# Second expert stage: finished rows scattered by POOL into a table in token order, read back by plain DMAs

## Chip, cores and metric

One core of a Trainium2 chip runs the whole program in one launch. The metric is the device time of an execution in microseconds (us), the median of three runs. Everything is fp32 (matmul operands are split into a high and a low part).

## The reference, cut to what matters

x is 8 x 1024 tokens of 128 values. A mixture-of-experts layer, a state-space mixer and a second mixture-of-experts layer follow one another, each with a residual:

```python
x = x + 0.5 * ffn(layernorm(x), router_w, w_gate, w_up, w_down)
x = x + attn(layernorm(x), ...)          # the mixer: conv, scan over time, gate, projection
x = x + 0.5 * ffn(layernorm(x), router_w, w_gate, w_up, w_down)

def ffn(x, ...):                         # 8 experts, each token goes to 2 of them
    logits = xt @ router_w.T
    topk_vals, topk_idx = jax.lax.top_k(logits, 2)
    g = sigmoid(topk_vals); g = g / (g.sum(-1) + 1e-10)
    for e in range(8):
        ge = sum(where(topk_idx == e, g, 0), -1)
        out += ge[:, None] * ((silu(xt @ w_gate[e]) * (xt @ w_up[e])) @ w_down[e])
```

The change concerns the last line of the program, the second ffn.

## The kernel before

A tile is 128 tokens, one on each partition; there are 64 of them, and x lives in SBUF (`x_sb`, its normed form in `xn_sb`). Three blocks follow each other: `first_stage` (first expert layer), `mixer`, `last_stage` (second expert layer, from 983 us on).

An expert layer works on groups of tiles. `LAYER2` has four groups of 24, 16, 16 and 8 tiles. For each group the router finds each token's two experts and gives both copies of the token a row in a buffer in DRAM where the rows of an expert lie together, in slots of 128 rows (`x_dispatched`). POOL writes the rows there by indirect DMAs (`Router.scatter`, L605: two a tile, each 128 rows of 512 B). The experts then work on pairs of slots (`Experts`), 28, 20, 20 and 12 pairs a group, 80 in all; the last pair of a group has one slot, so there are 156 slots. Slots are padded: 156 x 128 rows hold 16384 tokens' copies.

A step i of `pe_step`, `act_step` and `dve_step` is a software pipeline: gate and up matmuls of pair i (L714 to L716), silu (ACT L744), the product (DVE L770), turning the hidden rows of pair i - 1 (PE L724, ACT L751, DVE L778), turning the input rows of pair i + 2 (PE L703, ACT L758, DVE L785), the down matmuls of pair i - 2 (L736, L737) and its output rows (ACT L764, DVE L793 in `out_rows`). SP loads the input rows of a pair into one of four buffers (L664, it runs some five steps ahead of PE) and stores the finished rows to `y_dispatched`, still in expert order (L669, two buffers `yr`). Each engine runs its own queue strictly in order.

When all pairs of a group are stored, `Combine` brings the rows back: for each tile POOL issues two gathers (L380), one for each expert of its tokens, each 128 rows of 512 B by the row numbers in `row`; DVE adds each times its gate to x (L388, L391). Tile t may be gathered when tile t - 2 has landed and tile t - 4 has been added, and no sooner than `FETCH[t]`: pair 34 for tile 0, one tile a pair after that, so 46 tiles fall due before pair 80 and the rest after it. SP stores x to `out` in eight pieces of eight tiles, all of them queued behind its last store of output rows (L1752).

In `last_stage` POOL's queue is: the x scatters of groups 2 and 3 (24 tiles, 48 DMAs, one tile a pair from pair 10), then the 128 gathers. The same scatters of groups 0 and 1 are done in `mixer`.

## Time and profile before

| | us |
|---|---|
| median of 3 runs (lowest, highest) | 1322.62 (1321.95, 1323.84) |
| the profiled execution | 1321.73 |
| its span in the trace | 1320.0 |

| busy in the span | PE | DVE | ACT | POOL |
|---|---|---|---|---|
| us | 1078.9 | 901.4 | 768.8 | 540.9 |
| share | 82% | 68% | 58% | 41% |

The profile lists the busy time of each engine, the span cut into slices, the chain of work that ended last, and groups of instructions. A line number such as L605 is that of the kernel before. The whole-span shares say little here, since the three blocks have different limits; the trace is read by stretches. The silu of a pair (L744) marks its step: one silu a pair, so its start times are the pace of the expert loop. Pair 10's starts at 1028.01, pair 41's at 1131.01, pair 61's at 1198.68 and the last one, pair 79's, at 1258.61.

### The profile page before, as it was taken

Reading aid. Unit: us, or ns where it says so; the run is one execution under the profiler, and the core shown is the slowest. Engines: PE = TensorE matmul, PEld = TensorE weight load, DVE = VectorE, ACT = ScalarE, POOL = GpSimd, SP = SyncE. Lnnn points to the kernel's source line nnn. Section 1 sums busy time; section 2 is a strip of 40 time slices with the busy share of each in tenths; the row PEclk is TensorE's granted clock in tenths of the full one; section 3 lists DMA queues with packets and bytes.
Section 4 is the critical chain, followed back from the end, with each engine's and each line's share of the span. In section 5 each row is a group of like instructions: output and inputs, shape, how many; then the busy total and the mean of one; then the engine's idle time right before and its main releaser. Section 6 shows DMA issues by size and latency. Waiting matters only on the chain. (4 is left out here: it accounts for less than half of the span.)

```text
span 1320.0 us, 23316 instructions
## 1 busy us (share of the span) xinstructions
PE 1078.9 (82%) x6351; PEld 898.4 (68%) x6351; DVE 901.4 (68%) x2699; ACT 768.8 (58%) x1987; POOL 540.9 (41%) x595
## 2 busy tenths in 40 slices
PE   3578989998988999989989878986858999898820
PEld 3467877877866777767767666764637878777720
DVE  7667677768634778786868677567856775777742
ACT  5345655545548786877777747765625665454510
POOL 3615445654023333332223235530630465555565
PEclk9979999999989999999989889997879999999965
DMA  8535354444240000000000000001232344444352
GB/s 263 168 118 196 118 167 141 146 139 133 67 159 21 17 19 18 19 15 15 17 13 17 13 21 33 28 21 41 96 144 61 98 120 124 115 116 114 105 159 74
DMA packets 134330, 114.41 MB, mean 87 GB/s; under 512 B 15424, under 2 KB 118336, under 8 KB 134080
## 3 DMA queue, kind: packets, MB, share of 16 engines
q1 hardware_dynamic: 108864, 64.71, 16.4%
q0 software_dynamic: 16384, 33.59, 8.6%
q10 hardware_dynamic: 8960, 14.63, 3.2%
q8 instruction: 59, 0.97, 0.3%
q14 instruction: 63, 0.52, 0.1%
HBM read 52.90 MB, written 59.97 MB: 86 GB/s over the span
## 5 line engine op out<-in xcount | busy, mean ns | idle before, releaser
L605 POOL DMA_INDIRECT x_dispatched<-xn_sb,row x256 | 250.5, 979 | 259.5 <-DVE row L569 110.4
L380 POOL DMA_INDIRECT f_y_in<-y_dispatched,row x160 | 151.3, 946 | 115.1 <-issue 56.0
L953 POOL TENSOR_TENSOR x_skip<-tok,d_skip 128x256 f32<-128x256 f32 x64 | 40.9, 640 | 318.3 <-DVE y L1385 174.0
L1002 PE MATMUL bank<-xT_high,wc_high 128*128 128x512 f32 x256 | 129.3, 505 | 3.8 <-DVE xT_low L1311 3.1
L380 POOL DMA_INDIRECT y_in<-y_dispatched,row x96 | 95.1, 991 | 37.3 <-issue 19.8
L1002 PE MATMUL bank<-xT_high,wc_low 128*128 128x512 f32 x256 | 104.1, 407 | 0.0
L1002 PE MATMUL bank<-xT_low,wc_high 128*128 128x512 f32 x256 | 104.1, 407 | 0.0
L770 DVE TENSOR_TENSOR f_hf<-f_sg,banks 128x512 f32<-128x512 f32 x84 | 56.3, 670 | 61.5 <-issue 30.5
L736 PE MATMUL bank<-shared,f_hh 128*128 x326 | 92.5, 359 | 0.1
L744 ACT ACTIVATE f_sg<-banks 128x512 f32<-128x512 f32 x84 | 49.1, 585 | 70.8 <-PE banks L716 56.9
L1370 DVE TENSOR_TENSOR state<-state_decayed,bank 128x256 f32<-128x256 f32 x56 | 23.6, 421 | 91.4 <-PE bank L1071 88.1
L736 PE MATMUL bank<-shared,e_hh 128*128 x312 | 84.7, 348 | 0.0
L1193 ACT ACTIVATE da_masked<-upto,da 128x128 f32<-128x128 f32 x256 | 81.2, 392 | 0.7 <-DVE da L1337 0.7
L770 DVE TENSOR_TENSOR e_hf<-e_sg,banks 128x512 f32<-128x512 f32 x80 | 53.7, 671 | 40.8 <-ACT e_sg L744 21.7
L744 ACT ACTIVATE e_sg<-banks 128x512 f32<-128x512 f32 x80 | 47.2, 590 | 57.0 <-PE banks L716 37.3
L1069 PEld LDWEIGHTS bank<-x_dt,mix 128*128 128x128 f32 x512 | 74.3, 210 | 5.0 <-issue 1.0
L714 PE MATMUL banks<-shared,f_xh 128*128 x163 | 74.0, 454 | 2.9 <-DVE f_xl L785 1.3
L724 PE MATMUL bank<-ident,f_hf 128*128 128x128 f32 x326 | 52.9, 286 | 27.6 <-DVE f_hl L778 21.5
L737 PE MATMUL bank<-shared,f_hl 128*128 x326 | 75.2, 231 | 0.0
L1053 PE MATMUL banks<-da_masked,after 128*128 128x512 f32 x128 | 72.3, 649 | 1.7 <-ACT da_masked L1193 1.7
L724 PEld LDWEIGHTS bank<-ident,f_hf 128*128 128x128 f32 x326 | 41.0, 147 | 46.1 <-issue 23.1
L1069 PE MATMUL bank<-x_dt,mix 128*128 128x64 f32 x512 | 70.9, 286 | 0.0
(281 smaller groups left out, 3370.6 us busy)
## 6 DMA issues: line engine op xcount, KB each, us to landing
f_xr<-x_dispatched SPq DMA_DIRECT2D x79, 128.0 KB
y_dispatched<-f_yr SPq DMA_DIRECT2D x79, 128.0 KB
e_xr<-x_dispatched SPq DMA_DIRECT2D x76, 128.0 KB
y_dispatched<-e_yr SPq DMA_DIRECT2D x76, 128.0 KB
w_split<-shared ACTq DMA_DIRECT2D x8, 768.0 KB
shared<-w_split SPq DMA_DIRECT2D x8, 768.0 KB
x_dispatched<-xn_sb,row POOLq DMA_INDIRECT x256
out_dram<-x_sb SPq DMA_DIRECT2D x8, 512.0 KB
```

What stands on the lines that cost most here:

```text
L380: nc.gpsimd.indirect_dma_start(out=self.y_in[n % 4][k][:], out_offset=None, in_=self.rows[t], in_offset=bass.IndirectOffsetOnAxis(ap=row[k ...
L605: nc.gpsimd.indirect_dma_start(out=xd_dram[g.x_home], in_=xn_sb[:, t, :], in_offset=None, out_offset=bass.IndirectOffsetOnAxis(ap=row[k][: ...
L714: pe.matmul(to, high, w[:, 0:2 * H], start=True, stop=False)
L724: last = pe.transpose(b_h[:, (2 * u + c) * P:(2 * u + c + 1) * P], self.hf[i % 2][:, u, c * P:(c + 1) * P], ident[:])
L736: pe.matmul(to, self.hh[i % 2][:, 2 * u + c, :], w[:, at:at + 2 * D], start=(c == 0), stop=False)
L737: last = pe.matmul(to[:, 0:D], self.hl[i % 2][:, 2 * u + c, :], w[:, at:at + D], start=False, stop=(c == 1))
L744: nc.scalar.activation(self.sg[i % 2][:, 0:n, :], b_gu[i % 2][:].rearrange("p (u f) -> p u f", u=2)[:, 0:n, 0:H], ACT.Silu).then_inc(self. ...
L770: nc.vector.tensor_tensor(self.hf[i % 2][:, 0:n, :], self.sg[i % 2][:, 0:n, :], b_gu[i % 2][:].rearrange("p (u f) -> p u f", u=2)[:, 0:n, ...
L1002: last = pe.matmul(acc[:], wc[w][:, tap, k * P:(k + 1) * P], xTb[x][:, at:at + 512], start=(tap == 0 and i == 0), stop=(tap == CONV_K - 1 ...
L1053: pe.matmul(b_seg[:], after[:], dam[t % 2][:].rearrange("p h i -> p (h i)"), start=True, stop=True).then_inc(s_sg, 1)
L1069: pe.matmul(b_y[:, h * HD:(h + 1) * HD], mm[i][:, h, :], xdt[i][:, h, :], start=True, stop=True)
L1193: last = nc.scalar.activation(dam[t % 2][:, h, :], upto[:], ACT.Copy, scale=da[b % 2][:, c, h:h + 1])
```

## The change

Nothing changes in what is computed. In the second expert stage:

- Each row of `xn_sb` and of `x_dispatched` is 130 values wide instead of 128 (`XW`), in the first stage too. Column 128 holds 2 x token - 4N and column 129 the number of the expert that is the token's first choice, both written by two more DVE instructions a group in `choose`; they are zero in the first stage and in padding rows.
- When a pair's input rows are in SBUF, `targets` (two DVE instructions on 128 x 2 values, the second waits for the first) computes for each row its place in a table `y_by_token` of 2N rows: 2 x token + (1 if this expert is the token's first choice). Padding rows get a place beyond the table.
- `send` replaces the store by SP: POOL scatters the finished rows of each slot into the table, one indirect DMA a slot with a bounds check that drops rows beyond the table: 156 DMAs. Pair i's wait for its targets, its finished rows and the landing of pair i - 2's. There are four `yr` buffers instead of two; `out_rows` of pair i waits for the landing of pair i - 4's.
- The x scatters of groups 2 and 3 stand in POOL's queue between the sends: 16 tiles over steps 10 to 41, 8 tiles over steps 41 to 61.
- `Gathered` replaces `Combine`: SP reads the table in token order by 32 plain DMAs of 256 KB (two tiles each, four buffers), no gathers; DVE does the same two additions a tile. Before pair 80 come 55 tiles, one a step from step 34 on and two a step in steps 75 to 80; the 8 tiles of the last group and tile 55 come after the loop.
- `out` is stored piece by piece within SP's queue, not all at the end.

```diff
-                    last = nc.scalar.activation(xn_sb[:, t, :], x_sb[:, t, :], ACT.Identity,
+                    last = nc.scalar.activation(xn_sb[:, t, 0:D], x_sb[:, t, :], ACT.Identity,
...
                 if k == 0:
+                    if self.by_token:
+                        c(nc.vector.tensor_copy(xn_sb[:, tiles, D], token2[:, tiles]))
+                        c(nc.vector.tensor_scalar(xn_sb[:, tiles, D + 1], work2, -1.0, E + 1.0, ALU.mult, ALU.add))
...
             def load(self, sp, i):
                 need(sp, self.s_tr, i - XB + 1)
+                if self.router.by_token:
+                    need(sp, self.s_to, 2 * (i - XB + 1))
...
+            def targets(self, dve, i):
+                dve.wait_ge(self.s_xr[i % XB], 16 * (i // XB + 1))
+                if i >= 2 * YB:
+                    dve.wait_ge(self.s_yo[i % YB], self.sent(i - 2 * YB))
+                n = self.live(i)
+                rows = self.xr[i % XB]
+                if i:
+                    dve.wait_ge(self.s_to, 2 * i)
+                nc.vector.tensor_tensor(self.first[:, 0:n], rows[:, 0:n, D + 1], self.router.slotf[:, 2 * i:2 * i + n], ALU.is_equal
+                                        ).then_inc(self.s_to, 1)
+                dve.wait_ge(self.s_to, 2 * i + 1)
+                nc.vector.scalar_tensor_tensor(out=self.to[i % (2 * YB)][:, 0:n], in0=rows[:, 0:n, D], scalar=float(NOWHERE),
+                                               in1=self.first[:, 0:n], op0=ALU.add, op1=ALU.add).then_inc(self.s_to, 1)
+
+            def send(self, pool, i):
+                pool.wait_ge(self.s_to, 2 * i + 2)
+                pool.wait_ge(self.s_y, i + 1)
+                if i >= 2:
+                    pool.wait_ge(self.s_yo[(i - 2) % YB], self.sent(i - 2))
+                for u in range(self.live(i)):
+                    nc.gpsimd.indirect_dma_start(out=y_token, in_=self.yr[i % YB][:, u, :], in_offset=None,
+                                                 out_offset=bass.IndirectOffsetOnAxis(ap=self.to[i % (2 * YB)][:, u:u + 1], axis=0),
+                                                 bounds_check=2 * N - 1, oob_is_err=False
+                                                 ).then_inc(self.s_yo[i % YB], 16)
...
             def out_rows(self, dve, i):
                 dve.wait_ge(self.s_ylow, i + 1)
-                need(dve, self.s_yo[i % 2], 16 * (i // 2))
+                if not self.router.by_token:
+                    need(dve, self.s_yo[i % 2], 16 * (i // 2))
+                elif i >= YB:
+                    dve.wait_ge(self.s_yo[i % YB], self.sent(i - YB))
...
                 if i + 2 < self.pairs:
                     self.x_low(dve, i + 2)
+                    if self.router.by_token:
+                        self.targets(dve, i + 2)
...
+        class Gathered:
+            def load(self, sp, n):
+                sp.wait_ge(self.s_both, self.ADDED + max(0, 2 * (n - self.BUFS + 1)))
+                at = 4 * P * n
+                sp.dma_start(self.y_in[n % self.BUFS][:], y_token[at:at + 4 * P, :].rearrange("(t p k) d -> p t (k d)", p=P, k=2)
+                             ).then_inc(self.s_back[n % self.BUFS], 16)
...
+            SETTLED = 4
+            AHEAD = 6
+            LANDING = 2
             FETCH = []
             for g in LAYER2:
+                for n in range(g.first // 2, g.end // 2):
+                    FETCH.append(max(g.pair_end + SETTLED, FETCH[-1] + (1 if g.index > 1 else 2) if FETCH else 0))
+            SENT = {}
+            for g, first, end in ((LAYER2[2], beside[0].known, LAYER2[2].pair - 7), (last, LAYER2[2].pair - 7, last.pair - 7)):
                 for t in range(g.first, g.end):
+                    SENT.setdefault(first + (t - g.first) * (end - first) // g.tiles, []).append((g, t))
...
                 @block.gpsimd
                 def _(pool):
                     setup.wait_filled(pool, 6)
-                    for g in LAYER2[2:]:
-                        for t in range(g.first, g.end):
-                            r.scatter_paced(pool, ex, g, t, FIRST_SENT + t - LAYER2[2].first)
-                    for g in LAYER2:
-                        ex.wait_stored(pool, g.pair_end)
-                        for t in range(g.first, g.end):
-                            if FETCH[t] < PAIRS2:
-                                pool.wait_ge(ex.s_gu, FETCH[t] + 1)
-                            combine.pool(pool, t)
+                    for i in range(PAIRS2 + 2):
+                        for g, t in SENT.get(i, ()):
+                            r.scatter(pool, g, t)
+                        if i >= 2:
+                            ex.send(pool, i - 2)
```

## Rows read from the trace of the kernel before

**Rows 1.** Busy time by stretch, the last block: engine busy (instructions), clock, DMA share, GB/s.
```profile
core 0: us, PE busy (x) PEld busy (x) DVE busy (x) ACT busy (x) POOL busy (x), PEclk, DMA share, GB/s
985.00:1028.00 43.00, 37.20 (x231) 31.58 (x231) 28.66 (x96) 23.72 (x54) 0.00 (x0) 0.89 0.23 66
1028.00:1129.00 101.00, 96.38 (x635) 82.46 (x636) 71.35 (x174) 57.98 (x133) 57.35 (x60) 1.00 0.40 116
1129.00:1195.00 66.00, 58.80 (x380) 49.93 (x379) 48.43 (x116) 33.40 (x81) 36.96 (x40) 1.00 0.44 118
1195.00:1257.00 62.00, 55.91 (x362) 47.52 (x363) 46.39 (x112) 30.52 (x73) 34.98 (x37) 1.00 0.39 105
1265.56:1320.00 54.44, 0.00 (x0) 0.00 (x0) 13.88 (x40) 0.00 (x0) 32.30 (x35) 0.50 0.44 123
```

**Rows 2.** The chain that ended last, from 1250 us: its shares, and late pieces (start, us, what).
```profile
by line: issue 28.6%; DMA f_y_in<-y_dispatched,row 26.3%; POOL f_y_in L380 24.0%; another core or an unknown queue 4.4%; POOLq L1742 1.7%; DVE x_sb L391 1.0%; DVE e_hl L778 1.0%; PE bank L736 0.9%; ACT e_sg L744 0.9%; PE bank L724 0.9%; DVE
...
1267.35 5.04 DMA f_y_in<-y_dispatched,row
1274.37 4.98 DMA f_y_in<-y_dispatched,row
...
1313.19 2.43 DMA f_y_in<-y_dispatched,row
```

**Rows 3.** DVE in order of time: last output rows, last gathered tile.
```profile
1265.28 0.28 DVE L793 TENSOR_TENSOR e_yr<-bank,e_yl 128x128 f32<-128x128 f32 x1
...
1315.65 0.35 DVE L388 SCALAR_TENSOR_TENSOR x_sb<-f_y_in,gate,x_sb 128x128 f32<-128x128 f32 x1 [1.62 <-DMA f_y_in<-y_dispatched,row]
1316.04 0.35 DVE L391 SCALAR_TENSOR_TENSOR x_sb<-f_y_in,gate,x_sb 128x128 f32<-128x128 f32 x1
```

**Rows 4.** Groups of the last block (985 to 1320 us): busy, mean ns, idle before and releasers.
```profile
L380 POOL DMA_INDIRECT f_y_in<-y_dispatched,row x128 | 121.1, 946 | 85.2 <-issue 41.9 <-PE banks L716 16.6 <-DVE x_sb L391 15.1
L605 POOL DMA_INDIRECT x_dispatched<-xn_sb,row x48 | 46.0, 958 | 87.6 <-DVE row L569 56.9 <-PE banks L716 19.6 <-issue 9.1
```

**Rows 5.** POOL in order of time at the mixer's end: scatters back to back.
```profile
965.36 1.31 POOL L605 DMA_INDIRECT x_dispatched<-xn_sb,row  x1 [0.30 <-issue]
966.97 0.96 POOL L605 DMA_INDIRECT x_dispatched<-xn_sb,row  x1 [0.30 <-issue]
968.24 0.96 POOL L605 DMA_INDIRECT x_dispatched<-xn_sb,row  x1 [0.30 <-issue]
969.50 0.96 POOL L605 DMA_INDIRECT x_dispatched<-xn_sb,row  x1 [0.30 <-issue]
970.76 0.96 POOL L605 DMA_INDIRECT x_dispatched<-xn_sb,row  x1 [0.30 <-issue]
972.02 0.95 POOL L605 DMA_INDIRECT x_dispatched<-xn_sb,row  x1 [0.30 <-issue]
```

**Rows 6.** First input rows of the last block: SP's issue, and who waited for them.
```profile
982.66 4.30 SPq L664 DMA_DIRECT2D e_xr<-x_dispatched  x5
985.87 0.69 PE L703 MATMUL bank<-ident,e_xr 128*128 128x128 f32 x2 [9.31 <-DMA e_xr<-x_dispatched]
```

**Rows 7.** GB/s in 40 slices of 8.4 us, 985 to 1320 us.
```profile
GB/s 79 34 63 81 66 97 108 111 125 96 128 127 119 127 102 140 127 104 104 117 127 113 134 112 110 112 131 104 120 103 112 70 92 160 314 72 55 102 55 86
```

**Rows 8.** DVE in order of time: one step with a tile's additions, no idle time.
```profile
1250.81 0.68 DVE L770 TENSOR_TENSOR e_hf<-e_sg,banks 128x512 f32<-128x512 f32 x1
1251.41 0.68 DVE L778 TENSOR_TENSOR e_hl<-bank,e_hh 128x512 fp32r<-128x512 f32 x1
1252.01 0.41 DVE L785 TENSOR_TENSOR e_xl<-bank,e_xh 128x256 fp32r<-128x256 f32 x1
1252.34 0.41 DVE L793 TENSOR_TENSOR e_yr<-bank,e_yl 128x256 f32<-128x256 f32 x1
1252.67 0.34 DVE L388 SCALAR_TENSOR_TENSOR x_sb<-f_y_in,gate,x_sb 128x128 f32<-128x128 f32 x1
1253.05 0.35 DVE L391 SCALAR_TENSOR_TENSOR x_sb<-f_y_in,gate,x_sb 128x128 f32<-128x128 f32 x1
```

**Rows 9.** ACT in order of time: the silus of pairs 10, 41 and 61.
```profile
1028.01 0.60 ACT L744 ACTIVATE e_sg<-banks 128x512 f32<-128x512 f32 x1 [0.30 <-PE banks L716]
...
1131.01 0.63 ACT L744 ACTIVATE e_sg<-banks 128x512 f32<-128x512 f32 x1
...
1198.68 0.60 ACT L744 ACTIVATE e_sg<-banks 128x512 f32<-128x512 f32 x1 [1.06 <-PE banks L716]
```

**Rows 10.** All L605 scatters of the program: duration, and waits for an earlier one's landing.
```profile
L605 POOL DMA_INDIRECT x_dispatched<-xn_sb,row x256: 952/958/1348, 22.1 to 1106.8; - x128
...
  DMA x_dispatched<-xn_sb,row: 11.2, 13
```

**Rows 11.** DVE in order of time: two dependent instructions on 128 x 4 values.
```profile
7.03 0.16 DVE L160 TENSOR_TENSOR f_newton<-f_rstd 128x4 f32<-128x4 f32 x1
7.22 0.16 DVE L161 SCALAR_TENSOR_TENSOR f_newton<-f_newton,f_var 128x4 f32<-128x4 f32 x1
```

**Rows 12.** ACT in order of time: three silus of the first expert stage.
```profile
349.00 0.60 ACT L744 ACTIVATE f_sg<-banks 128x512 f32<-128x512 f32 x1 [1.05 <-PE banks L716]
...
351.97 0.60 ACT L744 ACTIVATE f_sg<-banks 128x512 f32<-128x512 f32 x1 [1.06 <-PE banks L716]
...
354.94 0.60 ACT L744 ACTIVATE f_sg<-banks 128x512 f32<-128x512 f32 x1 [1.06 <-PE banks L716]
```

**Rows 13.** Busy time of the first stretches, for DMA share: all work, first 60 us.
```profile
0.00:30.00 30.00, 11.05 (x53) 9.84 (x53) 21.73 (x132) 15.72 (x38) 7.81 (x22) 1.00 0.93 284
30.00:60.00 30.00, 12.36 (x72) 10.15 (x73) 19.22 (x59) 11.71 (x28) 19.10 (x19) 0.99 0.54 178
```

**Rows 14.** POOL in order of time: the program's first scatter.
```profile
22.05 1.14 POOL L605 DMA_INDIRECT x_dispatched<-xn_sb,row  x1 [18.38 <-DVE row L569]
```

More of the change, by code:

```diff
@@ L40 @@
 XB = 4
+YB = 4
+XW = D + 2
+NOWHERE = 4 * N
 fp32 = mybir.dt.float32
@@ L634, in __init__ @@
                 self.yl = [tb(f"yl{i}", [P, 2, D]) for i in range(2)]
-                self.yr = [tb(f"yr{i}", [P, 2, D]) for i in range(2)]
+                self.nyr = YB if by_token else 2
+                self.yr = [tb(f"yr{i}", [P, 2, D]) for i in range(self.nyr)]
                 self.s_w = None
@@ L649, in __init__ @@
                 self.s_y = sem(f"{tag}_out_rows")
-                self.s_yo = [sem(f"{tag}_out_stored{i}") for i in range(2)]
+                self.s_yo = [sem(f"{tag}_out_stored{i}") for i in range(self.nyr)]
+                if by_token:
+                    self.to = [tb(f"row_of{i}", [P, 2], i32) for i in range(2 * YB)]
+                    self.first = tb("is_first", [P, 2])
+                    self.s_to = sem(f"{tag}_row_of")
                 self.offsets = {}
@@ L673, in wait_stored, with sent, wait_sent @@
                     eng.wait_ge(self.s_yo[i], 16 * ((pairs + 1 - i) // 2))
+            def sent(self, i):
+                return 16 * sum(self.live(j) for j in range(i % YB, i + 1, YB))
+            def targets(self, dve, i):
[21 more added lines that the diff above has]
+                                                 ).then_inc(self.s_yo[i % YB], 16)
+            def wait_sent(self, eng, pairs):
+                for i in range(pairs - YB, pairs):
+                    eng.wait_ge(self.s_yo[i % YB], self.sent(i))
             def registers(self, pe, i):
```

102 lines of the change are left out of this document (64 added, 38 removed).

## The prediction

> **What bounds the kernel now.** I first cut the last block into stretches [rows 1]. Until 1257 us PE is busy 86% to 95% of the time: the expert loop is PE's, with POOL at about half. Behind 1265.56 PE does nothing at all, DVE is busy 13.9 of 54.4 us, and POOL 32.3 us. Then the chain that ended last [rows 2]: from 1250 us on it is POOL's gathers, the gathers' transfers and POOL's issue gaps, some 79% together. The last output rows of the experts are made at 1265.28 to 1265.56, the last tile is added at 1316.39, and its store lands at 1320.0 [rows 3]. So 54.4 us of the span are rows being fetched back, at the price of 0.95 us busy and 0.30 us gap for each gather [rows 4, 5]. That is what a plain read can take away. The reader should also see what the loop has to pay for it: the scatters go into a stretch in which PE runs on, and POOL's queue is strictly in order.
>
> **Part 1, the tail: minus 39 us.** Behind the last output rows at 1265.56 stand now 54.4 us. In their place come: one send of one slot, 1.26 us to issue [rows 5]; its landing; the first read; the rest of 1.5 MB (four reads of 256 KB, and the 512 KB store of the seventh piece, which SP has queued just before them); the additions of the last two tiles; the last store. Landing of a scatter is not in the trace. It is bounded by gathers and by the spacing of scatters: a gather lands 2.43 us after its issue began in quiet and 5.04 us with other traffic [rows 2], so 1.5 to 4.1 us behind the end of its issue; back to back, scatter n + 4 waits for the landing of n and starts 5.06 us after it (965.36 + 1.31 to the start at 970.76 is 4.09 us) with the ordinary gap of 0.30 [rows 5], so here a scatter landed within 4.1 us of its issue's end. I take 2.5, nearer to the quiet gather, for these DMAs are as large. The first read: 3.2 us from SP's issue to PE's use for 128 KB [rows 6]. 1.5 MB at 314 GB/s, the fastest slice [rows 7], are 5 us, of which 1.5 lie in the 3.2; at the 123 GB/s of the present tail [rows 1] they would be 12. Two tiles, four additions of 0.38 us [rows 3, 8], are 1.5. Store: 3.6 us, from 1316.39 to 1320.0 [rows 3]. Sum: 1.3 + 2.5 + 3.2 + 3.5 + 1.5 + 3.6 = 15.6, so about 39 us saved; the bounds are 32 (slow reads) and 42.
>
> **Part 2, POOL's queue in the loop: plus 10 us.** From step 10 to step 61 POOL has 48 x scatters and 102 sends less the two single slots of pairs 27 and 47, about 148 DMAs. At 1.26 us each [rows 5], 0.96 busy and 0.30 gap, these are 186.5 us. The loop takes 170.7 us for the same steps, 1028.01 to 1198.68 [rows 9]. So POOL falls behind by 15.8 us, 14.2 of it up to step 41 (93 DMAs, 117.2 us, in 103.0). Until its lag reaches PE something gives: `out_rows` of pair i waits for pair i - 4's landing, four steps of 3.34 us are 13.4, less the issue of two sends 2.5 and the landing 2.5, leaves 8.4 us. The rest, 7.4 us, stops DVE inside its step, before the next product, and through it PE. Steps are uneven (some 1.5 us, some 6), and POOL, when it has caught up for a moment, can't use a short one later: I add 2.5 and take 10. Waiting behind a late send in POOL's queue are the x scatters of groups 2 and 3, and behind those SP's first load of pair 48 and 68; the last of the scatters has its place 7 steps ahead of the group, and with a lag of four steps it still lands before PE turns those rows. From step 61 to 80 POOL has 38 DMAs, 48 us, in 60: it catches up, so the tail finds it free. Bounds: a scatter's cost with a bounds check and on finished rows isn't in the trace. Rows beyond the table, 3584 of 19968, move nothing; if that shortened the issue to 1.15 us, the 170 us would fit and the term be 0. The other way the longest scatter of the program took 1.35 us busy [rows 10], 1.65 with its gap: 244 us, a term of 65 to 70. I take 1.26, since 256 scatters have a median of 0.958 and 128 gathers a mean of 0.946 [rows 4, 10]: the direction makes no difference, and the count of rows is the same. At a landing of 4.1 instead of 2.5 the allowance shrinks by 1.6 and the wait of send i for send i - 2 begins to cost: 16 in all.
>
> The wait for the landing is also where a page speaks. The Trainium skill, DMA: Bandwidth & Descriptors, section on the anatomy of one DMA on the gpsimd path, puts some 2.0 us of every such DMA down to fixed cost, most of it the receipt of the write, heaviest for HBM. For 64 KB its fit gives an estimate of 2.15 us, by which this part would stay at 10.
>
> **Part 3, DVE: plus 5 us.** `targets` is two dependent instructions on 128 x 2 values. On 128 x 4 values such a pair starts 0.19 us apart and each is busy 0.16 [rows 11], so 0.4 us a step. They stand between x_low and `out_rows`. A full step with a tile's additions is 2.5 us of back-to-back work [rows 8], from the 1250.81 to the end of the additions at 1253.4; PE's is 2.97 in a stretch of the first expert stage in which PE never idles [rows 12]. 2.9 still fits, barely, and DVE was idle for a quarter of the loop (71.4, 48.4 and 46.4 us busy in 101, 66 and 62) [rows 1]; most is hidden by that, and where DVE is late after a stall it is not: 2 us, bounds 0 and 10. Six steps, 75 to 80, add two tiles: 2.5 + 0.7 + 0.4 = 3.6 us against 3.0 to 3.3, so 3 us. The number of additions is the same as before.
>
> **Part 4, small things: plus 2 us.** Two more instructions a group in `choose`, 0.2 each, four groups, half on a path: 1 us. Rows of 520 B in place of 512: 1.6% more bytes in fills, scatters and loads. In the last block the DMA share is 0.23 to 0.44 [rows 1] and they hide; in the first 30 us it is 0.93 [rows 13], so there they count, 0.5 to 1 us. SP's input loads are issued behind one more wait, for `targets` of four pairs back, one of DVE's instructions later; with four buffers that is one step of slack in four. POOL's setup grows by two small instructions, and it waits 18.38 us for DVE anyway before its first scatter [rows 14]. Taken out with no gain: SP's stores of finished rows (80 in the loop), SP is not late; the traffic of the loop falls, since scatter and read of 8 MB each replace a store of 10 MB and gathers of 8 MB.
>
> A rule speaks against the wider rows. The Trainium skill, DMA: Bandwidth & Descriptors, section on how a descriptor splits into AXI transactions, says that a descriptor that doesn't start on a multiple of 256 B fetches from the boundary below. A row of 520 B mostly starts so; the page makes the input rows up to some 30% dearer to move, an estimate. No run shows it yet; it would lengthen the 3.2 us of a hidden load and the first 30 us, by perhaps 3 us in all.
>
> **The sum.** On the profiled execution, 1321.73 us (span 1320.0): -39 + 10 + 5 + 2 = -22, 1299.7. It stands 0.9 below the median of the runs, so 1300.6; I say 1301.
>
> **Rivals.**
> (a) POOL doesn't bind: a step's PE stalls and POOL's issue overlap better, or dropped rows make a send shorter. Part 2 is 0 to 3 us. For it: the excess over the allowance is only 7 us in 171. Time 1292.
> (b) Landing or DVE is dearer: landings near 4.1 us as under traffic (16 instead of 10), reads in the tail at half the fast rate (+4), DVE's late steps (+3). For it: gathers took 5.0 us with stores beside them [rows 2], 13 scatters waited for a landing [rows 10]. Against: 243 didn't. Time 1314.
> (c) Slower: the send costs more than 1.42 us. Part 2 then is 148 x 1.42 = 210 less 171 and 8.4, plus 2.5, 33 us, which eats the 32 left of the gain. At 1.65 us, the dearest scatter seen, POOL bounds the whole loop: 244 us plus 3 behind step 61, a term of 70 and a time of 1361; between them, at 1.5, about 1335. For it: the bounds check is a new operation for POOL, and only 0.16 us are to spare. Against: the medians and means of 0.946 and 0.958 over hundreds of indirect DMAs [rows 4, 10].
> (d) It doesn't do what it says: SP, blocked at a table read or at the wait for a group's sends, starves the input loads, so the loop pays what the tail gives. The first table read waits for pair 27's send at SP's step 38, some five ahead of PE's 32 or 33, and with POOL four steps late it is blocked one or two steps, covered by the four input buffers. Five such waits of 3 us at most: 1316.
>
> **How the numbers follow.** The forecast 0.45 (1294 to 1308), (a) 0.22, (b) 0.15, (c) 0.12, (d) 0.06. The range holds 8 in 10 from below (a), with the tail's best bound 42 us, 1282, to where (c) begins, 1328. About 0.2%, 2.6 us, is what a measurement of this kernel can tell from no change. Faster is all but (c) and a little: 0.86; within it 0.02; slower 0.12.
>
> **What would show it.** Behind the last output rows some 15 us to the end, with reads of 256 KB and no gathers. POOL's sends 1.26 us apart, without idle time from about step 25 to step 60, and DVE's output rows waiting for the landing of a send; the last silu 12 to 17 us later than at 1258.61. Two DVE instructions of 0.16 us a step. The prediction is wrong if the sends are dearer than 1.3 us or cheaper than 1.2, if POOL idles in steps 30 to 60, or if the tail is longer than 20 us because reads queue behind a store.

## The result and the profile after

The changed kernel is slower: 1368.64 us, median of 4 runs (1367.95 to 1370.31), beside 1322.28 us for the kernel before (4 runs, 1315.32 to 1323.84). The ratio is 1.036, 95% interval 1.033 to 1.040. Said in advance were 1301 us and a range up to 1328. The profiled run has a span of 1367.0 us against 1320.0.

First the stretches, cut at silus as in [rows 9]. Windows of after (us, then busy time of each engine, granted clock, DMA share, GB/s), and ACT in order of time at the silus of pairs 10, 41 and 61 and the last:

```profile
core 0: us, PE busy (x) PEld busy (x) DVE busy (x) ACT busy (x) POOL busy (x), PEclk, DMA share, GB/s
1027.00:1188.00 161.00, 117.88 (x647) 98.53 (x646) 85.62 (x252) 61.06 (x139) 93.09 (x95) 0.85 0.25 70
1188.00:1281.00 93.00, 68.28 (x390) 57.67 (x388) 54.65 (x154) 34.46 (x81) 52.08 (x53) 0.89 0.37 104
```

```profile
1027.36 0.60 ACT L795 ACTIVATE e_sg<-banks 128x512 f32<-128x512 f32 x1 [0.28 <-PE banks L767]
...
1187.86 0.60 ACT L795 ACTIVATE e_sg<-banks 128x512 f32<-128x512 f32 x1 [2.28 <-PE banks L767]
...
1280.71 0.60 ACT L795 ACTIVATE e_sg<-banks 128x512 f32<-128x512 f32 x1 [0.39 <-PE banks L767]
...
1341.49 0.38 ACT L795 ACTIVATE e_sg<-banks 128x256 f32<-128x256 f32 x1 [0.36 <-PE banks L767]
```

| stretch of the last block | before, us | after, us | difference |
|---|---|---|---|
| first silu to pair 10 | 36.6 | 36.3 | -0.3 |
| pair 10 to pair 61 | 170.7 | 253.4 | +82.7 |
| pair 61 to the last silu | 59.9 | 60.8 | +0.9 |
| last silu to the end | 61.4 | 25.5 | -35.9 |

Up to the first silu there is no difference (991.42 before, 991.10 after), so the four rows make up the 47 us of the spans. The tail gave what it should. Everything else sits in pairs 10 to 61, where the prediction had +15. The windows say something more: PE is busy 118 of 161 us and 68 of 93 where it was busy 96 of 101 and 59 of 66 [rows 1], and its granted clock is 0.85 and 0.89 where it was 1.00. POOL isn't full either: 145 us busy in 254. With a gap of 0.3 us for each of the 148 DMAs the queue needs 191, so some 63 us are left over.

So who is late? POOL's sends and DVE's `targets`, all of them in the last block (ns minimum/median/maximum):

```profile
L717 POOL DMA_INDIRECT y_by_token<-e_yr,e_row_of x156: 982/985/1093, 1001.8 to 1351.7; - x156
...
L705 DVE TENSOR_TENSOR e_is_first<-e_xr,r_slotf x80: 148/151/213, 987.0 to 1339.2; 128x2 f32<-128x2 f32 x76, 128x1 f32<-128x1 f32 x4
```

Both cost nearly what was forecast (0.96 busy for a send, 0.16 for a target). The waits of ACT are what grew. First before (985 to 1260 us), then after (985 to 1345): who waited, what ended the wait, us in total, times, longest us. "remote" is the profile's word for another core or a queue that it doesn't know. The program runs on one core; the word means here that the last releaser that could be found had been done for over 1.5 us when the wait ended:

```profile
ACT e_yl L764 <- remote: 24.9, 12, 3.0
...
ACT e_sg L744 <- remote: 12.4, 8, 2.5
```

```profile
ACT e_yl L815 <- remote: 35.4, 19, 4.7
...
ACT e_sg L795 <- remote: 25.3, 11, 5.3
ACT e_hh L802 <- remote: 22.8, 12, 3.7
...
ACT e_xh L809 <- remote: 7.2, 6, 1.7
```

All "remote" waits of ACT come to 42 us before and 95 us after. In the chain that ended last they are the largest item of the changed stretch: "another core or an unknown queue" has 31.0% of after from 1027 to 1281 us (79 us), and 9.2% of before from 1028 to 1199 (16 us). First after, then before:

```profile
by line: another core or an unknown queue 31.0%; issue 11.0%; PE bank L787 8.6%; PE banks L767 7.8%; PE bank L775 7.7%; PE banks L765 6.7%; PE banks L766 5.9%; PE bank L754 3.9%; PE bank L788 3.8%; DVE e_hl L829 3.5%; ACT e_hh L802 2.4%; AC
by line: issue 14.3%; PE bank L736 10.7%; PE bank L724 9.9%; another core or an unknown queue 9.2%; PE banks L714 9.2%; PE banks L716 8.6%; PE banks L715 7.7%; DVE e_hl L778 4.9%; PE bank L737 4.6%; PE bank L703 3.6%; DVE e_yr L793 2.7%; DV
```

One of these waits in order of time (after, PE, POOL and ACT; the line of PE is the last matmul into the bank that L815 reads):

```profile
1032.88 0.39 ACT L809 ACTIVATE e_xh<-bank 128x256 fp32r<-128x256 f32 x1
...
1033.41 0.23 PE L788 MATMUL bank<-shared,e_hl 128*128 x1
...
1034.59 1.00 POOL L717 DMA_INDIRECT y_by_token<-e_yr,e_row_of  x1 [0.30 <-issue]
...
1035.89 0.99 POOL L717 DMA_INDIRECT y_by_token<-e_yr,e_row_of  x1 [0.30 <-issue]
...
1037.18 0.97 POOL L615 DMA_INDIRECT x_dispatched<-xn_sb,row  x1 [0.30 <-issue]
1037.95 0.38 ACT L815 ACTIVATE e_yl<-bank 128x256 f32<-128x256 f32 x1 [4.68 <-remote]
...
1042.26 0.38 ACT L490 ACTIVATE r_xT<-bank 128x256 f32<-128x256 f32 x1 [3.93 <-remote]
```

The bank is full at 1033.64, ACT has nothing before L815 in its queue, and yet L815 starts at 1037.95. PE then stands for 2.7 us up to 1039.04, for its down matmuls wait for DVE's output rows, and these come from L815. POOL meanwhile issues ten indirect DMAs without a break, 1029.36 to 1042.02.

The trace also records when each semaphore rises, and these records say where the time lies. The count that L815 waits for rises at 1037.92, 4.3 us after the end of the matmul that raises it, and ACT starts 0.02 us behind the rise. It is the same in all the "remote" waits of over 1 us that ACT has in the block, 35 after and 21 before: the count rises 1.5 to 8.9 us behind the end of PE's instruction, and ACT starts less than 0.1 us behind the rise. The ends of matmuls are modelled, but where ACT waits for PE on a chip without such waits (before_again, below) the rise comes 0.01 to 0.02 us behind them. So ACT isn't slow to start. PE's report reaches it late. I call this the stall.

Before, POOL has 20 runs of four in the block (DMAs with gaps of 0.5 us at most), and 17 of them hold a "remote" wait of ACT, mostly of some 2 us; its 27 runs of two hold one. These waits begin 2 to 5 us into the run and nearly all end within 1.1 us of its last DMA's end. After, sends and x scatters join to runs of up to ten, and 78 of the 95 us lie in runs of four or more; there the waits begin up to 12 us into a run, and a third of them end over 1 us before the run does. ACT isn't held up by the fetching of code: the DMA view of 1029 to 1043 us shows no packet of the instruction queues, and of the 35 waits of over 1 us in the block 25 have none inside.

### The profile page after: what moved, and what is told of

It is laid out like the page before. It is cut to its first block and busy times, and to the rows that moved or that the text cites. A ratio compares the mean times of both kernels' runs of the same rounds, so it can differ in the third digit from the quotient of the medians.

```text
span 1367.0 us, 23694 instructions
## 1 busy us (share of the span) xinstructions
PE 1106.7 (81%) x6351; PEld 916.7 (67%) x6351; DVE 924.0 (68%) x2867; ACT 771.3 (56%) x1987; POOL 578.0 (42%) x625
## 5 line engine op out<-in xcount | busy, mean ns | idle before, releaser
L717 POOL DMA_INDIRECT y_by_token<-e_yr,e_row_of x156 | 154.5, 991 | 163.9 <-issue 118.5
L775 PE MATMUL bank<-ident,e_hf 128*128 128x128 f32 x312 | 54.2, 300 | 65.6 <-DVE e_hl L829 50.3
L775 PEld LDWEIGHTS bank<-ident,e_hf 128*128 128x128 f32 x312 | 40.6, 155 | 87.9 <-issue 51.6
L787 PE MATMUL bank<-shared,e_hh 128*128 x312 | 90.6, 366 | 5.2 <-DVE e_yr L847 5.1
L787 PE MATMUL bank<-shared,f_hh 128*128 x326 | 88.8, 349 | 4.0 <-DVE f_yr L847 3.9
L765 PE MATMUL banks<-shared,e_xh 128*128 x156 | 72.8, 467 | 2.1 <-issue 1.2
```

The costliest lines, as they stand in the source:

```text
L717: nc.gpsimd.indirect_dma_start(out=y_token, in_=self.yr[i % YB][:, u, :], in_offset=None, out_offset=bass.IndirectOffsetOnAxis(ap=self.to[ ...
L765: pe.matmul(to, high, w[:, 0:2 * H], start=True, stop=False)
L775: last = pe.transpose(b_h[:, (2 * u + c) * P:(2 * u + c + 1) * P], self.hf[i % 2][:, u, c * P:(c + 1) * P], ident[:])
L787: pe.matmul(to, self.hh[i % 2][:, 2 * u + c, :], w[:, at:at + 2 * D], start=(c == 0), stop=False)
```

## The experiments

The kernels ran on several chips, and the chips differ: the kernel before takes 1319 to 1332 us on two of them (7 and 10, as on that of the result), and 1266 to 1270 us on two others (13 and 11), where ACT has no "remote" wait at all. I call the first ones stalling and the second ones quiet. Every comparison below is with the kernel before on the same chip; the changed kernel itself ran on chip 13 and on that of the result, not on 7, 10 or 11.

**The parts one by one, on chip 13.** Four kernels: all rows of the sends dropped, with the table reads taken from x instead; the sends as plain DMAs of POOL; the sends as plain DMAs of SP; and the kernel before with its gathers all behind the loop. The first three don't bring the rows to their tokens. The edits, cut:

```diff
--- a_all_dropped: POOL issues every send, no row is written
-  in0=rows[:, 0:n, D], scalar=float(NOWHERE),
+  in0=rows[:, 0:n, D], scalar=float(2 * NOWHERE),
...
-  at = 4 * P * n
+  at = 4 * P * n % N
...
--- a_pool_plain
-  nc.gpsimd.indirect_dma_start(out=y_token, in_=self.yr[i % YB][:, u, :], in_offset=None,
+  nc.gpsimd.dma_start(y_token[at + u * P:at + (u + 1) * P, :], self.yr[i % YB][:, u, :])
--- a_sp_store: the same on the sync queue, eight steps behind the input loads
+  nc.sync.dma_start(y_token[at + u * P:at + (u + 1) * P, :], self.yr[i % YB][:, u, :])
...
-  r.scatter(pool, g, t)
+  r.scatter_paced(pool, ex, g, t, i)
--- b_no_gather_in_loop (kernel before)
-  if FETCH[t] < PAIRS2:
-      pool.wait_ge(ex.s_gu, FETCH[t] + 1)
+  pool.wait_ge(ex.s_gu, PAIRS2)
```

> The changed kernel, but every row's place lies beyond the table, so POOL issues all 156 sends as before and no row is moved; the table is read from x instead (left out: the rows never reach their places). In the changed kernel the last silu starts at 1341.5 us and ACT waits 94.7 us in all, between 985 and 1345 us, for something that no record of the profile explains. Theory 1, POOL's runs of indirect DMAs issued back to back hold ACT up, whatever they move: nothing changes, last silu at 1335 to 1345, those waits 80 to 100 us. Theory 2, the scattered rows' traffic and landing does it: last silu at 1262 to 1280, those waits under 45 us. Theory 3, POOL's queue alone bounds the loop, as predicted: unchanged too, but then POOL would not be idle for 164 us beside its sends.

> The changed kernel with the sends as plain DMAs issued by POOL, slot after slot in expert order, same sizes, count and waits (left out: the rows are not brought to token order). Theory 1 in the narrow form, only indirect DMAs do it: ACT's unexplained waits fall under 45 us and the last silu comes at 1265 to 1285. Theory 1 in the wide form, any run of DMAs issued by POOL: waits stay over 70 us and the last silu behind 1320. Theory 2 (scattered writes): like the narrow form.

> The changed kernel with the rows stored by SP by plain DMAs, slot after slot in expert order (left out: token order), and the x scatters, which are all that POOL has left, paced by the gate and up matmuls as before. targets on DVE, the wider rows, the waits and the plain table reads stay. If POOL's sends cost the loop its 83 us (theories 1 to 3): last silu at 1255 to 1265 and the end 20 to 25 us behind it, 1278 to 1290 in all. If DVE's targets or the wider rows cost a part (theory 4): last silu at 1275 or later.

> The kernel before with all 128 gathers of the second layer behind the loop; in the kernel before 93 of them are issued before the last output rows, in runs of four and two. Theory 1: the loop from pair 37 on gets quicker, from 3.32 us a pair to 3.0 to 3.15, last silu at 1243 to 1252 instead of 1258.6, and ACT's unexplained waits behind pair 33 fall from 36 us to under 5. Theories 2 in part likewise (less traffic). If POOL's issues have nothing to do with ACT: last silu at 1257 to 1260 and waits of over 30 us. The total gets longer by some 90 to 115 us in any case, the moved gathers at 1.25 us each.

Measured, one run each: 1275.4, 1240.1, 1238.1 and 1376.5 us, the kernel before 1267.2. No kernel showed a single "remote" wait of ACT, so this chip couldn't tell the cause of the stall. It told the size of the rest. Pairs 10 to 61 take 185.5 us with all rows dropped, 158.9 with POOL's plain DMAs (0.55 us each), 158.9 with SP's, and 156.3 in the kernel before without gathers, where PE is busy 154 of 156 us: that is PE's own pace. The indirect sends of POOL cost 27 us there, and 186.1 with rows written (after_again, below) beside 185.5 with none says that it makes no difference whether rows move.

**Both kernels again on chip 13, with two repeats.**

> The changed kernel unchanged. Where ACT shows no unexplained waits (as in the four runs before this one, in which the kernel before took 1267 us): POOL's queue alone binds, the loop like that of the run with all rows dropped (last silu 277 us behind the first), end 25 us behind it: 1272 to 1282, 1.00 to 1.015 of the kernel before. Where ACT shows them (as in the first traces of both kernels): 1.03 to 1.04 of the kernel before at some 1322 us.

> The kernel before unchanged, for its trace on this chip. If ACT's unexplained waits are what parts 1322 from 1267 us: at 1267 they are absent and the last silu is 245 to 250 us behind the first; at 1322 they are 40 to 60 us in all and the last silu is 265 to 270 us behind the first.

> As the run with stores by SP, on a chip that may show ACT's waits. If POOL's runs of back-to-back indirect DMAs bring them on (theory 1): even there they are under 15 us from pair 2 on, for POOL has only pairs of x scatters, and the last silu is at most 262 us behind the first. If they come with the chip whatever POOL does: 40 us and more.

> As the run with all rows dropped, on a chip that may show ACT's waits. There: theory 1 (issuing does it, whatever is moved): 80 to 100 us of them and the last silu 340 to 355 us behind the first, as in the changed kernel. Theory 2 (the rows' writes do it): under 40 us, last silu 275 to 290 us behind the first. Without ACT's waits: as before, 277 us.

After 1271.7 us (10 runs) and before 1269.5 (13 runs), ratio 1.001, interval 0.9995 to 1.003: here the change is a tie. The repeats gave 1241.7 and 1270.6. The spans of the profiled pair (1271.9 and 1264.4) split so: up to the first silu +6.0, to pair 10 +1.2, pairs 10 to 61 +29.8 (156.3 to 186.1), to the last silu +3.4, tail -33.0. Where the 29.8 go is in the waits of after_again, 1003 to 1190 us, and in POOL's queue, which has one unbroken run of 107 indirect DMAs and no stall:

```profile
DVE e_is_first L705 <- issue: 32.5, 20, 4.0
```

```profile
1076.43 0.96 POOL L615 DMA_INDIRECT x_dispatched<-xn_sb,row  x1 [0.31 <-issue]
1077.69 1.00 POOL L717 DMA_INDIRECT y_by_token<-e_yr,e_row_of  x1 [0.30 <-issue]
1079.00 1.00 POOL L717 DMA_INDIRECT y_by_token<-e_yr,e_row_of  x1 [0.30 <-issue]
1080.30 0.98 POOL L717 DMA_INDIRECT y_by_token<-e_yr,e_row_of  x1 [0.30 <-issue]
1081.59 0.98 POOL L717 DMA_INDIRECT y_by_token<-e_yr,e_row_of  x1 [0.30 <-issue]
1082.88 0.97 POOL L615 DMA_INDIRECT x_dispatched<-xn_sb,row  x1 [0.30 <-DMA y_by_token<-e_yr,e_row_of]
```

`targets` of pair i + 2 and `out_rows` of pair i - 2 both wait for the landing of send i - 6, and `targets` stands first in the step: that is DVE's 32.5 us. The profile names no releaser for them ("issue"), but the chain of the same window goes through the sends, their landings and the x scatters:

```profile
by line: issue 30.7%; DMA y_by_token<-e_yr,e_row_of 18.0%; POOL y_by_token L717 17.9%; POOL x_dispatched L615 6.8%; PE bank L787 2.8%; DVE e_xl L836 2.4%; DVE e_yr L847 2.3%; PE bank L775 2.0%; PE banks L765 2.0%; PE banks L767 1.8%; PE ban
```

In a_sp_store_2 these waits are missing and PE is busy 96.7 of 100 us:

```profile
1003.00:1103.00 100.00, 96.74 (x644) 83.89 (x644) 82.21 (x250) 60.55 (x137) 31.01 (x32) 1.00 0.43 114
```

**More buffers, and the wide rows alone, on chip 10.** Eight `yr` buffers instead of four; the same with the x scatters 9 to 11 steps earlier; and the kernel before with rows of 520 B.

```diff
--- c_eight_buffers
-YB = 4
+YB = 8
--- c_eight_early, besides
-            SETTLED = 4
+            SETTLED = 8
-            for g, first, end in ((LAYER2[2], beside[0].known, LAYER2[2].pair - 7), (last, LAYER2[2].pair - 7, last.pair - 7)):
+            for g, first, end in ((LAYER2[2], beside[0].known, LAYER2[2].pair - 16), (last, LAYER2[2].pair - 16, last.pair - 18)):
--- b_wide_rows (kernel before)
+XW = D + 2
```

> The changed kernel with eight buffers for finished rows (and 16 for their places) instead of four; out_rows of pair i waits for the landing of pair i - 8's. Where ACT has no unexplained waits: if POOL's queue is the bound, four more steps of lag (4 x 3.1 us) are worth about 12 us of the loop from pair 10 to 61 (186.1 us in the changed kernel, here 172 to 176), and the end is then held by POOL's last send: 188 DMAs of 1.29 us behind pair 10's silu and 14 us of tail give 1258 to 1263, 0.990 to 0.995 of the kernel before. If DVE's two instructions or SP were the bound: no change, 1270 to 1273.

> As with eight buffers, and the x scatters of groups 2 and 3 stand earlier in POOL's queue (steps 10 to 32 and 32 to 50 instead of 10 to 41 and 41 to 61), the first table read of a group 8 steps behind its last pair instead of 4. POOL's total is the same, so if its queue bounds the end: 1257 to 1263 as well. If late x scatters (SP's and PE's waits for a group's first rows) cost the version with eight buffers something: this one is 3 us or more quicker.

> The kernel before with rows of 130 values in xn_sb, x_dispatched and the fills, and nothing else of the change. The last block began 4 us later in the changed kernel's runs on this chip than in those of the kernel before (965.3 against 960.9 us, means of six and two). If the wider rows do that: 2 to 5 us slower than the kernel before, ratio 1.002 to 1.004, and the DMA share from 70 to 366 us is 0.03 to 0.04 higher at nearly the same GB/s. If not: ratio within 0.999 to 1.001.

Ratios 1.036 (1.032 to 1.039), 1.033 (1.030 to 1.037) and 0.998 (0.995 to 1.001). On this chip the stall is there ("remote" waits of ACT in the block 93, 100 and, with the wide rows alone, 56 us), so what was expected of the two kernels with eight buffers on a quiet chip stays untested. Here twice the buffers seem to win nothing, by their ratios of 1.036 and 1.033 beside the 1.036 of the changed kernel on its own chip. POOL stood idle for 178 us before the sends of c_eight_buffers, so its backlog isn't what limits there. The wide rows alone cost nothing that can be measured in the time.

**What in POOL's runs holds ACT up, on chip 7.** Three kernels of above again, and the kernel before with a rest of POOL, waited for, before each pair of indirect DMAs:

```diff
--- b_pause (kernel before), before the two scatters and before the two gathers of a tile
+  nc.gpsimd.wait_ge(self.s_pause, self.paused)
+  nc.gpsimd.memset(self.pause[:], 0.0).then_inc(self.s_pause, 1)    # 128 x 1024
+  nc.gpsimd.wait_ge(self.s_pause, self.paused + 1)
```

> The changed kernel with every row of its output sends out of bounds, so that POOL issues the same indirect DMAs and no output row is written; the table loads read x instead. Output not the reference's. On a chip with the stall: theory 1a (issuing on POOL holds ScalarE up): waits of ScalarE about 95 us, time within 1% of after's ratio of 1.036. Theory 1b (the data that the rows write does it): waits fall to about the 42 us of before or less, time 1300 us or less. On a chip without it: 1272 us, as seen.

> The changed kernel with its output sends as plain DMAs on the sync queue, rows in slot order, so that the scatter by token is left out and the output is not the reference's; POOL keeps the scatters of x alone. On a chip with the stall: theory 1 (POOL's runs): runs of two at most, waits of ScalarE under 15 us, the loop at 165 us or less, and with the short tail of after about 1280 to 1295 us in all. Rival 3 (the number of row writes in flight, whoever issues them, holds ScalarE's inputs up): waits of ScalarE stay above 60 us and the time above 1340 us. On a chip without it: 1240 us, as on the first two looks.

> The changed kernel with its output sends as plain DMAs on POOL's queue, rows in slot order (the scatter by token is left out, output not the reference's); 0.55 us each on POOL instead of 0.99. On a chip with the stall: if any DMA of POOL counts, waits of ScalarE about 50 to 95 us and a time of 1320 us or more; if indirect ones alone count, runs of two remain and it comes out at 1280 to 1295 us with waits under 15 us. On a chip without it: 1242 us, as seen.

> The kernel before, with POOL made to rest (a memset of 1024 elements per partition, waited for) before the two row scatters of each tile and before the two gathers of each tile in the last block's loop, so that its runs of four indirect DMAs become two and two; nothing is left out. On a chip where ScalarE stalls (before above 1315 us): theory 1 (a run of more than some three indirect DMAs on POOL holds ScalarE up): ScalarE's unexplained waits in the loop fall from 42 us to under 15 and the kernel gets faster by 10 to 25 us. Rival 2 (the DMAs themselves cost it, however they are spaced): the waits stay at about 42 us and the time within 0.4%, or longer by the pauses. On a chip without the stall (before about 1267 us): within 0.3% of before by both.

| kernel on chip 7 | us | ratio (interval) | pairs 10 to 61, us | "remote" waits of ACT in them, us |
|---|---|---|---|---|
| a_all_dropped_3 | 1369.1 | 1.036 (1.031 to 1.041) | 254.4 | 74 |
| a_sp_store_3 | 1265.2 | 0.957 (0.951 to 0.962) | 159.8 | 1.9 |
| a_pool_plain_3 | 1264.0 | 0.957 (0.953 to 0.962) | 158.8 | 0 |
| b_pause | 1322.8 | 1.002 (0.999 to 1.005) | 169.3 | 0 |

The longest "remote" waits of ACT in a_all_dropped_3 (985 to 1346 us), then all of a_sp_store_3 (985 to 1250):

```profile
ACT e_yl L815 <- remote: 29.9, 14, 5.0
ACT e_sg L795 <- remote: 28.0, 10, 5.2
ACT e_hh L802 <- remote: 16.0, 11, 2.5
```

```profile
ACT r_xT L490 <- remote: 1.9, 1, 1.9
```

The data of the rows has nothing to do with it: without any row written the stall stays, and with 254.4 us the stretch is as long as the 253.4 of the changed kernel (theory 1a; 1b falls). POOL's DMAs as such don't bring it on either: in a_pool_plain_3 POOL issues two scatters and two plain sends without a break, and no "remote" wait follows. Indirect DMAs in unbroken runs do. Both kernels with plain sends came out faster than the 1280 to 1295 us said for them.

b_pause shows that the break matters and not the number. From pair 41 to 61 POOL issues 40 gathers in 68.4 us there and 41 in 67.7 us in the kernel before; before, ACT has 15.3 us of "remote" waits in that stretch, in b_pause none. Its 29 waits under "issue" at the silu (985 to 1260 us) are 1.1 us each, the wait of an ordinary step [rows 12]. The "remote" waits of before from 1131 to 1199 us:

```profile
ACT e_yl L764 <- remote: 9.8, 4, 3.0
...
ACT e_sg L744 <- remote: 5.5, 3, 2.5
```

POOL in b_pause, 1122 to 1191 us, and its chain in the same window:

```profile
L380 POOL DMA_INDIRECT f_y_in<-y_dispatched,row x40 | 38.0, 949 | 11.5 <-POOL pause L445 5.4 <-DVE x_sb L391 4.0 <-issue 2.1
L445 POOL MEMSET pause<- 128x1024 f32 x21 | 20.4, 971 | 0.0
```

```profile
by line: DMA f_y_in<-y_dispatched,row 44.2%; issue 17.7%; POOL f_y_in L380 14.9%; POOL pause L445 9.9%; DVE x_sb L391 6.8%; DVE x_sb L388 6.8%; DVE e_hl L788 1.0%; DVE e_xl L795 0.5%; DVE e_yr L803 0.5%; POOLq L444 0.2%
```

The forecast of its time missed all the same (I had 10 to 25 us less). With a rest of 0.97 us a tile needs 3.44 us of POOL, 20 tiles 68.8, the 68.4 measured. The chain agrees: it goes through the gathers and the pause, and DVE waits 17.0 us for gathers to land, of which the kernel before has none in these pairs. So the pause became the bound that the stall had been. Ahead of the last block, where there are no rests, ACT keeps 30 us of such waits.

"remote" counts a late rise only from 1.5 us on. The semaphore records give the rest: summed over ACT's waits in pairs 10 to 61, the part that lies between the end of PE's instruction and the rise is 38 us in the kernel before, 84 in the changed one, 72 in a_all_dropped_3, 10 in b_pause (none over 1.04 us), and 6 in a_pool_plain_3 and in a_sp_store_3. On the quiet chips no rise that ACT waits for in these pairs is later than 0.02 us in any kernel, the run of 107 included. So rests and plain DMAs take away most of the lateness on a stalling chip, and not all. And the runs themselves seem to be in part made by it: on the quiet chip POOL of the kernel before has 52 runs of two and six of four, where on the stalling one it has 27 and 20, though the program is the same.

**A shorter rest, on chip 11.** The rest cut to 128 x 256 values, in the kernel before and in the changed one, there before each pair of DMAs (`a_break`) or once a step (`a_break_four`).

> The kernel before with the rest on POOL cut from 1.0 us to about 0.25 us (a memset of 256 elements per partition, waited for) before each pair of indirect DMAs in the last block's loop; nothing is left out. POOL then needs 2.7 us per tile, under the 2.9 us of a step. On a chip with the stall (before above 1315 us): if runs without a break are the cause and a short break ends them, ScalarE's waits fall from about 42 us to under 10, pairs 41 to 61 take 58 to 61 us instead of 68, and the time is 1290 to 1303 us. If what counts is the number of such DMAs per stretch, the waits stay above 30 us and the time within 0.4% of before. On a chip without the stall: within 0.3% of before.

> The changed kernel with the same short rest before each pair of indirect DMAs (two x scatters of a tile, two sends of a pair). 148 DMAs at 1.27 us and 74 rests at 0.25 us make 207 us for pairs 10 to 61. With the stall: if runs are the cause, ScalarE's waits fall from about 95 us to under 15, pairs 10 to 61 take 205 to 212 us instead of 254, and the time is 1315 to 1330 us, about the time of before. If the number per stretch is the cause, the waits stay above 60 us and the time at 1365 to 1390 us. Without the stall: pairs 10 to 61 take 205 to 210 us instead of 186 and the time is about 1292 us.

> The changed kernel with one short rest per step of the loop, so that runs of up to four (sometimes six, where a step has two tiles) remain. With the stall: if runs are the cause and those of four cost about 2 us each, as in the kernel before, ScalarE's waits come out between the two, 40 to 70 us, and the time between 1330 and 1355 us. If the number per stretch is the cause, 85 us or more and 1360 us or more. Without the stall: about 1282 us.

This chip has no stall, so whether a short break cures it stays open. b_break: 1266.4 us, ratio 0.999 (0.998 to 1.0005), as both theories had for this case. a_break 1332.4 us, 1.051 (1.047 to 1.055), and a_break_four 1311.4, 1.036 (1.032 to 1.040), both dearer than the 1292 and 1282 said for it. But they measure POOL's queue as the bound: 74 rests make pairs 10 to 61 228.6 us, 42 more than in after_again, 0.57 each. A rest is 0.35 busy, and the gap behind it is 0.78 before a send (0.28 before an x scatter), where 0.30 is usual. DVE's wait in `targets` (L713 here) grows with it from 32.5 us, 1005 to 1234 us of a_break:

```profile
DVE e_is_first L713 <- issue: 82.8, 36, 5.4
```

## Why the prediction was wrong

**Part 1, the tail, was right.** Forecast -39, bounds 32 and 42, measured -35.9, and -33.0 on chip 13, near the lower bound. Behind the last output rows at 1349.34 there are 17.7 us instead of the 15.6 of the sum. DVE's last rows and the two long pieces of the chain:

```profile
1349.34 0.28 DVE L847 TENSOR_TENSOR e_yr<-bank,e_yl 128x128 f32<-128x128 f32 x1
...
1351.69 3.33 DMA y_by_token<-e_yr,e_row_of
...
1355.17 2.87 DMA e_y_in<-y_by_token
```

Two sends stand before the last one in POOL's queue, so it starts 2.35 us after the rows that it carries. From its start to its landing are 3.33 us, of which 0.98 are its issue: 2.35 behind the issue's end, where I took 2.5. The Trainium skill, DMA: Bandwidth & Descriptors, section on the anatomy of one DMA on the gpsimd path, gave an estimate of 2.15 for a DMA of this size, its setup included. This row agrees within 0.2 only when it is counted from the end of the issue; the x scatters of after_again landed a median of 2.5 us behind the start of theirs. The first read took 2.9 us (3.2). Eight tiles were added at the end and not two, 5.3 us for the 3.5 of the other reads and the 1.5 of the additions. One reading of this part is off without effect: in [rows 5] the fifth scatter starts 5.40 us behind the first, not 5.06; the 4.09 that bounds the landing is right.

**Part 2 failed, and it is two terms.** The step that failed first is "The loop takes 170.7 us for the same steps". I took this for the pace of PE, and so for the time that POOL's 186.5 us have to fit in. It held 28 us of "remote" waits of ACT; without them the loop takes 156.3 (before_again). The form of the sum was good: 148 DMAs at 1.29 us are 191 us, less 156.3 and the allowance of 8.4, plus 2.5, are 29, and the quiet chip measured 29.8 (27 of it POOL's indirect sends, by a_sp_store and a_all_dropped). The 10 in its place was 19 too small. The stalls were to be seen: 4.4% of the chain's shares in [rows 2] are "another core or an unknown queue", in a program on one core, and 9.2% of the stretch that the sum was about. I didn't ask what they were. (Behind step 61 POOL has 37 DMAs, not 38, for pair 67 has one slot; it changes nothing.)

The second term wasn't in the sum at all. In runs of POOL's indirect DMAs PE's reports reach ACT late on some chips, in the kernel before too, and the change makes the runs longer. ACT's "remote" waits in pairs 10 to 61 rise from 28 to 85 us; against the quiet chip the stretch is 14.4 us longer before (170.7 and 156.3) and 67.3 after (253.4 and 186.1). That is +53. PE waits more, and its granted clock over the two windows is 0.85 and 0.89, a mix of its levels of 1.2 and 2.4 GHz, where before had 1.00 and after_again 0.98 and 0.96; what the lower clock adds to its matmuls isn't separated from the 53. The stretch grew by 82.7, of which 29.8 are there on the quiet chip too and 52.9 are not, against the forecast of 10 + 5. That the 52.9 are the stall and not another difference of the chips is shown by a_sp_store_3 and a_pool_plain_3. They keep the waits for landings, the additions and the table reads, have next to no stall, and take 159 to 160 us on a stalling chip, as their twins do on the quiet one.

"POOL idles in steps 30 to 60" was named as a sign that the prediction is wrong, and it came (the 63 us above). A second sign, that DVE's output rows wait for the landing of a send, was right on chip 13, with `targets` one place earlier in the queue. The last silu came 83 us later and not 12 to 17.

**Part 3 and 4.** `targets` costs 0.15 and 0.16 us, as said. In a_sp_store_2 pairs 10 to 61 take 158.9 us with all of DVE's new work, 2.6 more than before: for the 5 of the sum that is within its bounds. The wide rows: b_wide_rows, 0.998 (0.995 to 1.001), so alone they cost 1.5 us at most. Even so the 2 us of Part 4 look too small. On the quiet chips the first silu of the block comes at 961.8 to 969.8 us in the eight traces of kernels with the whole change ahead of the block (mean 965.5) and at 959.7 to 962.1 in the three without (mean 960.6), and on chip 7 the kernels of the first kind are 5 to 9 us later than b_pause. That is some 5 us, about half of it there by the last silu of the first expert stage (343.3 and 340.6), while the result's pair shows none (991.1 and 991.4). No experiment took it apart. By the rule of the Trainium skill, DMA: Bandwidth & Descriptors, section on how a descriptor splits into AXI transactions, the input rows would be some 30% dearer to move, an estimate, and I made 3 us in all of it; the time of b_wide_rows doesn't show them. The DMA share of the first expert stage (before_again, then after_again, 70 to 200 us) rises by 0.03 at nearly the same bytes, 6% and not 30%, though only a part of the traffic is input rows:

```profile
70.00:200.00 130.00, 114.19 (x778) 100.54 (x779) 94.93 (x279) 77.23 (x183) 57.69 (x60) 0.93 0.49 156
```

```profile
70.00:200.00 130.00, 112.47 (x761) 98.94 (x762) 92.85 (x275) 75.56 (x179) 56.33 (x60) 0.93 0.52 154
```

**The rivals.** (c), the only one with a time near the result, had the wrong mechanism: it wanted sends above 1.42 us, and they take 1.29. (a) is contradicted by the 27 us of the queue. (b) asked for landings near 4.1 us, and the one on the chain landed 2.35 us behind its issue; on the chain of after_again none took more than 3.7 us with its issue. (d), starved loads, shows nowhere: in pairs 10 to 61 of after and after_again no engine waits for a load of input rows, and none stands on the chain.

**What stays open.** Why PE's report comes late: the trace shows when a semaphore rises and not what the update waits for. Whether a break of 0.3 us ends a run. What makes some chips stall and others not. Besides the time, one thing sets them apart: on the stalling ones 634 to 906 of the 5063 to 5231 updates that PE, ACT and DVE make to semaphores have no record in the trace, in b_pause and the kernels with plain sends too, and on the quiet ones 0 to 24. Every time here is of a run with a recorded span, so whether the recording takes part in the stall isn't tested. No version here that computes the reference beats the kernel before on a stalling chip. The two that do (0.957) leave the scatter by token out; they only say what is to be had if the finished rows leave POOL's indirect DMAs.

## What to carry to other kernels

A wait whose releaser had long been done is part of the measured time but of no engine's pace. Take it out before the time of a loop is used as room for something else, and look at what the other engines do in it; here it was an unbroken run of POOL's indirect DMAs, and the change made these runs longer. Work moved from the end of a program into a loop has to fit into the loop's fastest pace, counted with its gaps: 148 DMAs at 1.29 us don't hide in 156 us, whatever their data.

## What the runs showed of the hardware

- On chips 7 and 10, and that of the result, semaphore updates of PE reach ACT up to 9 us late while POOL issues some four or more indirect DMAs with gaps of 0.3 us, with rows written or dropped ("remote" waits of 85 us in pairs 10 to 61 of after, 74 in a_all_dropped_3). With plain sends or rests between pairs of them the waits are gone and the lateness is 6 to 10 us in all. On chips 13 and 11 none that ACT waits for is late by more than 0.02 us in these pairs, whatever POOL does. The kernel before takes 1319 to 1332 us on the first and 1266 to 1270 us on the second.
- An indirect DMA of 128 rows keeps POOL for 0.96 to 0.99 us and a gap of 0.30, with dropped rows as with written ones. The sends, which have a bounds check, take 0.985 at the median and the x scatters 0.962 (after_again). A plain DMA of 64 KB from POOL takes 0.55.
- Rows of 520 B instead of 512 made no difference in time (0.998, b_wide_rows).
